# When the query weights of a gated attention block are centred: ahead of block 0, or during its softmax

## The reference, cut to what matters

```python
# x: (2, 2048, 512), ctx_1024: (2, 77, 512); Wq, Wk, Wv, Wo: (512, 512); 16 heads of 32
def _layernorm(x, axis=-1, eps=1e-05):
    m = jnp.mean(x, axis=axis, keepdims=True)
    v = jnp.var(x, axis=axis, keepdims=True)
    return (x - m) / jnp.sqrt(v + eps)
...
q = (query @ Wq.T).reshape(b, sq, H, HD).transpose(0, 2, 1, 3)
k = (key @ Wk.T).reshape(b, sk, H, HD).transpose(0, 2, 1, 3)
v = (value @ Wv.T).reshape(b, sk, H, HD).transpose(0, 2, 1, 3)
scores = jnp.where(causal[None, None], jnp.einsum('bhqd,bhkd->bhqk', q, k) * SCALE, NEG)
out = jnp.einsum('bhqk,bhkd->bhqd', jax.nn.softmax(scores, axis=-1), v)
out = out.transpose(0, 2, 1, 3).reshape(b, sq, d) @ Wo.T
...
x = x + jnp.tanh(g_xattn[0]) * _L0_xattn_ref(_layernorm(x, axis=-1), ctx_1024, ctx_1024, Wq, Wk, Wv, Wo)
x = x + jnp.tanh(g_ffn[0]) * _L0_ffn_ref(_layernorm(x, axis=-1), w_gate, w_up, w_down)   # SwiGLU, hidden 1536
```

## Time and profile before

| | |
|---|---|
| median of three runs | 907.96 us |
| profiled execution, its own time | 910.43 us |
| its span | 908.6 us |
| PE busy | 865.1 us, 95% |
| DVE busy | 643.1 us, 71% |
| ACT busy | 435.8 us, 48% |
| POOL busy | 427.5 us, 47% |
| share of the last-ending chain on PE | 76% |

### The profile page before, as it was taken

One profiled execution on the slowest core, in us unless ns is written; L12 is line 12 of the kernel. 1 busy time (PEld: TensorE's weight loads), 2 busy tenths in 40 slices (PEclk: granted clock), 3 DMA queues, 4 the chain that ended last, 5 costly groups with the idle time before them and its releaser, 6 DMA issues.

```text
span 908.6 us, 12903 instructions
## 1 busy us (share of the span) xinstructions
PE 865.1 (95%) x4089; PEld 712.7 (78%) x4089; DVE 643.1 (71%) x1090; ACT 435.8 (48%) x1130; POOL 427.5 (47%) x362
## 2 busy tenths in 40 slices
PE   4978999999999999899899999999999999999997
PEld 2757888888888887678688888888888878888876
DVE  3776868685868778759668747687567677477682
ACT  2565656555565656436406536246355165362450
POOL 5364767675767663146414524334534145242240
PEclk9999999999999999899999999999999999999999
DMA  6425373655546350526804327324256043262212
GB/s 199 151 61 177 114 232 128 195 163 161 176 153 218 116 207 12 203 73 235 307 0 144 135 86 275 126 82 157 93 202 233 2 158 119 97 219 79 82 41 94
DMA packets 61589, 129.53 MB, mean 143 GB/s; under 512 B 8416, under 2 KB 21216, under 8 KB 61536
## 3 DMA queue, kind: packets, MB, share of 16 engines
q1 hardware_dynamic: 61248, 128.85, 41.5%
q10 hardware_dynamic: 288, 0.00, 0.0%
HBM read 100.72 MB, written 27.80 MB: 141 GB/s over the span
## 4 chain that ended last, share of the span: by engine, by line
PE 76%; DVE 7%; POOL 5%; ACT 4%; issue 3%; SPq 3%; DMA 2%; ACTq 0%; POOLq 0%; DVEq 0%
PE psum L1705 30%; PE psum L1460 24%; PE psum L1755 18%; POOL xs L557 3%; PE psum L1494 3%; SPq L429 2%; POOL e L571 1%; DMA ring<-w_var 1%; POOL hT L680 1%; PE psum L1572 1%; ACT e L774 1%; DVE pT L998 1%; DVE x L1124 1%; DMA wq_stage<-wq_t 1%; ACT pT L745 1%
## 5 line engine op out<-in xcount | busy, mean ns | idle before, releaser
L1705 PE MATMUL psum<-xv,ring 128*128 128x512 f32 x1344 | 310.3, 392 | 5.1 <-DMA ring<-w_var 3.6
L1705 PEld LDWEIGHTS psum<-xv,ring 128*128 128x128 f32 x1344 | 252.1, 189 | 60.8 <-issue 4.2
L680 POOL TENSOR_TENSOR hT<-th,hT 128x512 fp32r<-128x512 f32 x48 | 85.1, 1772 | 221.0 <-ACT hT L937 221.0
L1755 PE MATMUL psum<-w_d,hT 128*128 128x512 f32 x768 | 177.6, 390 | 1.2 <-POOL hT L680 0.7
L1755 PEld LDWEIGHTS psum<-w_d,hT 128*128 128x128 f32 x768 | 143.6, 188 | 32.5 <-POOL hT L680 2.0
L571 POOL TENSOR_TENSOR e<-e,rden 128x616 f32<-128x616 f32 x64 | 77.9, 1217 | 115.2 <-DVE rden L1054 83.7
L1460 PE MATMUL psum<-xT,wq 128*128 128x512 f32 x384 | 96.5, 405 | 3.0 <-POOL xT L563 2.9
L1460 PE MATMUL psum<-wo,aT 128*128 128x512 f32 x384 | 95.1, 398 | 0.5 <-DVE aT L1014 0.5
L1340 DVE SCALAR_TENSOR_TENSOR acc<-psum,gate_ffn,acc 128x512 f32<-128x512 f32 x64 | 47.6, 749 | 65.5 <-PE psum L1755 65.4
L905 ACT ACTIVATE a<-psum 128x512 f32<-128x512 f32 x48 | 28.3, 590 | 125.6 <-PE psum L1705 125.6
L1460 PEld LDWEIGHTS psum<-xT,wq 128*128 128x128 f32 x384 | 72.4, 194 | 18.3 <-POOL xT L563 3.1
(11 more groups left out here) (105 smaller groups left out, 1220.7 us busy)
## 6 DMA issues: line engine op xcount, KB each, us to landing
ring<-w_var SPq DMA_DIRECT2D x48, 896.0 KB, 4.8
w_var<-stage SPq DMA_DIRECT2D x12, 896.0 KB, 5.0
x_ln<-x SPq DMA_DIRECT2D x32, 256.0 KB, 4.7
x_res<-x SPq DMA_DIRECT2D x32, 256.0 KB, 6.3
x_mid<-x_res SPq DMA_DIRECT2D x32, 256.0 KB, 2.0
x<-x_mid SPq DMA_DIRECT2D x8, 1024.0 KB, 8.9
acc<-x_mid SPq DMA_DIRECT2D x8, 1024.0 KB, 8.2
out<-acc SPq DMA_DIRECT2D x32, 256.0 KB, 2.0
```

The lines of the kernel that those rows point to most:

```text
L680: nc.gpsimd.tensor_tensor(hT[:, 1, i % HH, j, :], h[:, :], hT[:, 0, i % HH, j, :].bitcast(f32), ALU.subtract).then_inc(h_lo, 1)
L1705: last = nc.tensor.matmul(psum[:, bank, :], stat, mov, start=start and j == 0, stop=j == len(terms) - 1, skip_group_check=not start)
L1755: last = nc.tensor.matmul(m_bank[t % 2][:, :], hT[:, a, m, t // TT, (t % TT) * P:(t % TT + 1) * P], w_d[:, HH * h + m, :], start=m == 0 an ...
```

## The change

Wq goes into block 0 as it was loaded. The mean product moves into block 0 on PE, behind `batch_values(1)`, and into the other PSUM bank. DVE's four subtractions move behind `p(1, 2)` of block 0. ACT then makes the four high parts a second time, DVE the four low parts a second time, and `q(0)`, the first query product for block 1, waits for them. `wq_stage` now lies where `raw` lies, the landing place of the gate and up weights, so SP fetches those later: behind block 3's rows of x instead of ahead of the residual rows. POOL's split of Wo moves from ahead of block 0's softmax to behind it.

```diff
@@ SP
+                if first:
+                    sp.wait_ge(w_split, 2 * KD)
+                    fetch(1, 0)
+                    fetch(1, 1)
...
             sp.wait_ge(wo_split, 2)
-            fetch(1, 0)
-            fetch(1, 1)
@@ POOL: this loop stood ahead of rstd1(1)
             probabilities(0, 3)
+            for j in range(2):
+                pool.wait_ge(w_hi, KD + j + 1)
+                ks = slice(2 * j, 2 * j + 2)
+                nc.gpsimd.tensor_tensor(wo[:, 1, ks], x_res[:, ks, :], wo[:, 0, ks].bitcast(f32),
+                                        ALU.subtract).then_inc(wo_split, 1)
@@ ACT
+            for k in (0, 1):
+                split_hi(wq_in[k], wq[:, 0, k], wq_stage[:, k, :])
             x_high(0, 0)
             x_high(1, 1)
-            split_hi(wq_centred, wq[:, 0, 0], wq_stage[:, 0, :], 1)
-            split_hi(wq_centred, wq[:, 0, 1], wq_stage[:, 1, :], 2)
...
                 if first:
+                    act.wait_ge(m_full, 4)
+                    for k in range(KD):
+                        split_hi(wq_centred, wq[:, 0, k], wq_stage[:, k, :], k + 1)
                     v_high(0)
                     exp0(n, 3)
@@ DVE
-            dve.wait_ge(wq_mean, 1)
-            for k in range(KD):
-                dve.wait_ge(wq_in[k], 16)
-                nc.vector.tensor_tensor(wq_stage[:, k, :], wq_stage[:, k, :], m_bank[1][:, :], ALU.subtract)\
-                    .then_inc(wq_centred, 1)
...
+            def centre_wq():
+                dve.wait_ge(wq_mean, 1)
+                dve.wait_ge(w_split, KD)
+                for k in range(KD):
+                    nc.vector.tensor_tensor(wq_stage[:, k, :], wq_stage[:, k, :], m_bank[0][:, :], ALU.subtract)\
+                        .then_inc(wq_centred, 1)
...
                 p(1, 2)
+                if first:
+                    centre_wq()
...
                     denominator0(n, 3)
+                    for k in range(KD):
+                        wq_low(k, True)
                     q(0)
@@ PE
-            pe.wait_ge(avg_ready, 1)
-            for k in range(KD):
-                pe.wait_ge(wq_in[k], 16)
-            product(m_bank[1][:, :], [(avg[:, :], wq_stage[:, k, :]) for k in range(KD)]).then_inc(wq_mean, 1)
...
                     batch_values(1)
+                    pe.wait_ge(avg_ready, 1)
+                    pe.wait_ge(m_free, V_AT + 1)
+                    for k in range(KD):
+                        pe.wait_ge(wq_in[k], 16)
+                    product(m_bank[0][:, :], [(avg[:, :], wq_stage[:, k, :]) for k in range(KD)]).then_inc(wq_mean, 1)
                     p(0, 2)
...
                     pe.wait_ge(x_lo, 4)
+                    pe.wait_ge(w_split, 2 * KD)
                     q(0)
```

More of the change, by code:

```diff
@@ L144, in flamingo_gated_block @@
             raw = sb("raw", [P, 2, 2, KD, P], i32, a0)
+        with ExitStack() as a5:
+            sb("gap0", [P, 3 * KD * D + 2 * KD * TB + TT * D], f32, a5)
+            wq_stage = sb("wq_stage", [P, KD, D], f32, a5)
         with ExitStack() as a1:
@@ L182, in flamingo_gated_block @@
         with ExitStack() as c0:
-            wq_stage = sb("wq_stage", [P, KD, D], f32, c0)
+            sb("gap4", [P, KD, D], f32, c0)
             wk_stage = sb("wk_stage", [P, KD, D], f32, c0)
@@ L582, in _ @@
             nc.gpsimd.memset(v_full[:, :, :, :], 0.0).then_inc(v_zero, 1)
[L584 to L588, removed]
             rstd1(1)
@@ L779, in exp1 @@
                 last.then_inc(exp1_done, 1)
+            for k in (0, 1):
+                split_hi(wq_in[k], wq[:, 0, k], wq_stage[:, k, :])
             x_high(0, 0)
             x_high(1, 1)
-            split_hi(wq_centred, wq[:, 0, 0], wq_stage[:, 0, :], 1)
-            split_hi(wq_centred, wq[:, 0, 1], wq_stage[:, 1, :], 2)
+            for k in (2, 3):
+                split_hi(wq_in[k], wq[:, 0, k], wq_stage[:, k, :])
             x_high(2, 2)
             x_high(3, 3)
-            split_hi(wq_centred, wq[:, 0, 2], wq_stage[:, 2, :], 3)
-            split_hi(wq_centred, wq[:, 0, 3], wq_stage[:, 3, :], 4)
             act.wait_ge(k_zero, 1)
@@ L1083, in v_low_rows, with wq_low @@
                     .then_inc(v_split[b], 1)
-            def wq_low(k):
-                split_lo(k + 1, wq[:, 1, k], wq_stage[:, k, :], wq[:, 0, k])
-            dve.wait_ge(wq_mean, 1)
-            for k in range(KD):
-                dve.wait_ge(wq_in[k], 16)
-                nc.vector.tensor_tensor(wq_stage[:, k, :], wq_stage[:, k, :], m_bank[1][:, :], ALU.subtract)\
-                    .then_inc(wq_centred, 1)
+            def wq_low(k, again=False):
+                split_lo(k + 1 + (KD + 2 if again else 0), wq[:, 1, k], wq_stage[:, k, :], wq[:, 0, k])
+            def centre_wq():
[4 more added lines that the diff above has]
+                        .then_inc(wq_centred, 1)
+            wq_low(0)
+            wq_low(1)
             x_low(0, 0)
             x_low(1, 1)
-            wq_low(0)
-            wq_low(1)
+            wq_low(2)
+            wq_low(3)
             x_low(2, 2)
             x_low(3, 3)
-            wq_low(2)
-            wq_low(3)
             for m in range(G):
```

## The result

The changed kernel took 913.40 us, the median of five runs (911.77 to 915.56), against 907.96 us before (905.91 to 908.66). The ratio is 1.0064, with a 95% interval of 1.0052 to 1.0076: slower by 0.6%, as forecast (913.2 us).

The account below looks back on a forecast made before the run. PE is busy 95% of the span, so only block 1's start counts; Wq bounds the kernel's start. Block 1 7.7 later, plus 0.2 behind Wo, minus 2.7 front: 5.2 on 907.96, 913.2 us; forecast 911 to 915.5, bounds 908.8 to 917.5.

Parts of the forecast that it names:

- The front, forecast 2.7 us: Kernel start: PE no longer waits for the mean; queries 5.2 us earlier, less 2.5 for slow PE, gain 2.7 us.
- The order of the bounds: Kernel start: first transposes wait for POOL's tile 0, about 11.6; keys(0) then waits for Wk, landing at 13.94 us.
- the low clock: Kernel start: PE slow until 19, so 5.1 us of slow work instead of fast costs the front 2.5 us.
- The mean product, 3.4 us: Block 0 on PE, between batch_values(1) and p(0, 2): its 3.44 us delay what follows.
- The step that all of it passes on through DVE to tile 2's sums: Block 0: all 3.4 us of the mean product reach DVE, ACT's exponentials and tile 2's sums.
- Subtractions 2.5 us, low parts 2.5 us: Block 0 on DVE: four subtractions ahead of tile 3's shift, 2.48 us; four low parts before q(0), 2.5 us.
- The low clock before q(0), 0.7 us more than before: Block 0: after PE idles from about 61 to 70, q(0) takes 5.3 us instead of 4.62, 0.7 more.
- The slack of 1.88 us and ACT's high part: Block 0: q(0) may come 1.88 us later free; ACT's second high part at 76.4, 7.9 us late instead of 9.8.
- Wo's split as the last before block 1: POOL's 4.75 us split ends at 87.1; block 1 starts at 87.2, 7.7 us late, the split making 1.2.
- Behind Wo, forecast 0.2 us: Block 1: V's split hidden; chain over SP to x_scale 0.9 later with about 0.6 to spare; adds 0.2 us.
- The sign of being wrong: Prediction wrong if q(0) starts before about 64 on the new clock, or blocks 1 to 7 change their pace.
- The rival with POOL as the bound: Block 1's start: each split waits on DVE, or ACT held at V's split; 2 to 3 us more, 916 us; chance 0.15.

Follow-up runs that it names:

- run 10: Changed kernel with 36 superfluous unit-matrix products on PE ahead of its first transposes (warm start); ratio 1.0045, median 912.3 us.
- run 3: Changed kernel with the mean product behind block 0's last scores, subtraction behind tile 3's sum, high parts behind exp0; ratio 1.0044, median 912.5 us.
- Run 4: Changed kernel with 13 rounds of four superfluous score products in PE's idle time before q(0); ratio 1.0041, median 912.5 us.
- run 5: Kernel before with only POOL's split of Wo moved behind block 0's softmax; ratio 1.0061, median 913.2 us.
- run 2: Changed kernel with POOL's split of Wo back at its old place; ratio 1.0032, median 910.9 us.
- run 6: Kernel before with 24 superfluous unit-matrix products on PE ahead of the mean product (warm start); ratio 0.9975, median 905.1 us.
- run 1: Changed kernel without any recentring of Wq, so blocks 1 to 7 compute something else; ratio 0.9973, median 905.8 us.
- run 9: Kernel before with Wo's split late and SP's gate and up weight fetches behind block 3's rows of x; ratio 1.0017, median 910.3 us.

## Why the prediction was right

The side, the size and the mechanism of block 0 held, and on the clock of before q(0), ACT's high part and the start of block 1 came out to about 0.1 us. But the sum owes its accuracy to errors that cancel. Times of the changed kernel are put on the clock of before by adding 4.34.

- **The front, forecast 2.7 us, was 4.3.** Queries at 20.14 and not 21.8. The order of the bounds was right (POOL's rows, then Wk), and run 10 confirms 19.3 for a fast PE. Mis-sized was the low clock: I let it last until 19, and it had ended by 16.2: the second transposes (16.22) are already at full pace. It cost 0.9 us there (20.14 - 19.20), up to 2 in other executions of the same front, not 2.5. How early PE starts to be fast also moves the kernel before: the unchanged front gave 24.48, 23.48 and 22.90 us. So one profile fixes this term to no better than a microsecond.
- **The mean product, 3.4 us: right** in length (3.43), and tile 2's shift was late by as much (49.87 + 4.34 - 50.76 = 3.45). The step that all of it passes on through DVE to tile 2's sums was too strict. The small scaling behind it took 0.17 us, and 1.21 in run 3 where the product does not stand there (before: 1.05). Moved against POOL's work, DVE got about 1.2 us back over tiles 2 and 3, where I had allowed 0.2.
- **Subtractions 2.5 us, low parts 2.5 us:** 2.47 as forecast, and 3.47, 1 us more. One of the four low parts ran beside POOL's probabilities and took 1.71 us, and these took 1.55 instead of 1.22 us; in run 3, with POOL idle, the four took 2.49. The two errors on DVE cancel, and q(0) came at 65.57 + 4.34 = 69.9 for 70.0. The Trainium skill (SBUF — State Buffer, Who interferes with whom) says that a VectorE instruction with two inputs in SBUF contends with a GpSimd instruction that reads SBUF. The low parts have two such inputs, and the trace agrees: 3.47 us beside POOL's work, 2.49 without.
- **The low clock before q(0), 0.7 us more than before: right.** 5.37 for 5.3 us. Run 4 shows that it is worth 2.4 us in all.
- **The slack of 1.88 us and ACT's high part: right,** 71.94 + 4.34 = 76.3 for 76.4.
- **Wo's split as the last before block 1: right.** PE waits for it, 0.61 us for 1.2, and block 1 starts at 87.28 for 87.2 on the clock of before.
- **Behind Wo, forecast 0.2 us, was 2.05.** From block 1's start to block 2's values it was 45.12 us before and is 47.17 now. This is the step that failed. Of the chain over SP I had said that it gets 0.9 us later with 0.6 to spare. From the chain that ended last in the changed kernel:

```profile
86.39 1.02 POOL rstd L545
...
87.49 1.53 DMA rs_row<-rstd
...
89.19 4.21 DMA rsb<-rs_row
```

Against the start of block 1, 1/std landed 1.06 us later than before: 0.57 because POOL came to 1/std later, right behind its two splits, and 0.5 because the two transfers took 1.53 and 4.21 us and not 1.4 and 3.8. p(0, 2) came 0.5 us late. That part was only under-sized. What I had put at nothing is the clock: the idle time before p(0, 2) rose to 2.02 us, the granted clock fell, and a projection took 4.59 us instead of 3.01, 1.6 more. That the clock falls there is not certain: in runs 3 and 10, with 2.00 and 1.62 us of idle time at this place, the projection took 3.01. SP's queue has little to do with it here, since the 1/std transfer took nearly what it took before. That the fetches stand behind block 3's rows in the changed kernel, for the sake of the shared memory, spared it the larger loss of run 5, which I had not seen either.
- **The sign of being wrong.** I had written that the prediction is wrong if blocks 1 to 7 change their pace. Block 1 did, by these 2.05 us; blocks 2 to 7 did not.

The errors of 1.6 at the front and 1.85 behind Wo have opposite signs; with both the sum is 5.45 instead of 5.2. That the forecast of 913.2 us was met so closely is luck in this measure; each half alone would have missed by more than a microsecond and a half. The rival with POOL as the bound had the right place in part, since block 1 lost 2 us behind POOL's two splits, but neither of its two ways of losing them.

## What to carry to other kernels

Work that is taken off the head of a kernel must be looked up at its new place with the same care as what it frees: here 4.3 us were freed in a stretch where PE waited, and 6.7 us (run 2) put on the one path to the next block's queries. If an engine waits at the start anyway, heat it with superfluous work before moving necessary work away; 24 tiny products gained 2.3 us (run 6), as much as the rearrangement would have if recentring had cost nothing (2.5, run 1). And before a wait is moved to a later place on one engine, list what the DMA queue issues behind that wait, and which small transfer comes right after.

## What the runs showed of the hardware that I had not expected

- A transfer of 2 KB issued on SP's queue 0.9 us after the last of 2 MB of loads took 5.00 us to land (run 5). With 1 MB ahead of it, issued 3.1 us earlier, it took 1.50 (run 9) and 1.53 (changed). Run 9 shows that the order of the issues decides; whether the transfer waits in its queue or shares the engines with the loads is not shown.
- The scaling on DVE, 128 x 8 numbers, takes 0.17 us while POOL is idle. In these traces, where it begins early in an instruction of POOL, it ends when that does: at 54.25 beside 54.20 in the kernel before, at 51.22 beside 51.19 in run 3.
- A low clock follows shorter gaps than I had counted with: after 2.0 us of idle time before p(0, 2) the granted clock was 0.50 for 3.4 us in three profiles (changed, runs 4 and 9), and stayed at 1.00 after the same gap in run 3. Before p(3, 1) of block 0 it fell after 2.05 us of idle time in the kernel before and stayed at 1.00 after 2.36 in run 6. So the same gap may cost nothing, or 1.2 to 1.6 us in the product behind it. The busy time of the changed kernel by stretch, with PEclk the third number from the end:

```profile
16.00:17.00 1.00, 1.00 (x11) 1.00 (x10) 1.00 (x2) 0.30 (x2) 1.00 (x1) 1.00 0.02 6
...
66.00:67.00 1.00, 1.00 (x4) 0.71 (x4) 0.00 (x0) 0.00 (x0) 0.00 (x0) 0.50 1.00 377
...
102.00:103.00 1.00, 1.00 (x4) 0.81 (x3) 0.58 (x1) 1.00 (x8) 0.62 (x1) 0.50 0.03 8
```

- At a kernel's very start the listing gives a granted clock of 1.00 while matmuls run at half pace. The spacing of the matmuls shows the pace there, and run 6 confirms it: the eight matmuls that took 6.7 us take 3.67 when PE has been busy before them, at the same listed 1.00.
